# Fourteen filling products on TensorE ahead of the decoder of a four-layer conditioned network

## What is computed

```python
U = (mu @ W_dec + b_dec).reshape(B, IN_DIM + 1, K)      # mu 128x128, K = 30
param = jnp.einsum('bik,kj->bij', U, V)
weight, bias = param[:, :-1, :], param[:, -1, :]
x = x + jnp.einsum('bsd,bde->bse', x, weight) + bias[:, None, :]
x = x + clip(dcoefs * ((x * styles) @ weight.T) + bias)          # layer 1
x = x + relu(x @ w_down) @ w_up + x                              # layer 2, per entry
x = x + mlp_ln(concat(six normalised or shifted copies of x))    # layer 3
```

## Time and profile before

| | |
|---|---|
| three runs, median | 525.68 us |
| lowest and highest | 521.61 and 526.17 us |
| the profiled execution | 521.21 us |
| its span, first to last instruction | 519.4 us |
| mean granted clock of TensorE | 0.994 |

### The profile page before, as it was taken

The page is one execution under the profiler, slowest core; times in us unless marked ns, Lnnn a source line. Parts: engine busy times, 40 slices in busy tenths (PEclk is TensorE's granted clock), DMA queues, the critical chain, the costliest instruction groups (busy, mean ns, idle before and its releaser), DMA issues.

```text
span 519.4 us, 9425 instructions
## 1 busy us (share of the span) xinstructions
PE 486.3 (94%) x3198; PEld 354.2 (68%) x3198; DVE 405.8 (78%) x696; ACT 336.3 (65%) x638; POOL 391.0 (75%) x367
## 2 busy tenths in 40 slices
PE   2987887999999999999999999999999999998993
PEld 2953644767677776768686867677776768687682
DVE  2958876868788788888787878788787888886863
ACT  4573667456767676766777776767676767656832
POOL 6468799889878879697978787788779793787321
PEclk9999999999999999999999999999999999999997
DMA  8887705625252352608080716253442613104102
GB/s 299 247 304 208 203 20 124 163 73 135 83 127 81 77 171 56 191 24 223 0 229 17 205 43 173 74 136 112 106 142 63 175 47 90 49 21 145 40 2 81
DMA packets 34989, 61.78 MB, mean 119 GB/s; under 512 B 5017, under 2 KB 17413, under 8 KB 34580
## 3 DMA queue, kind: packets, MB, share of 16 engines
q1 hardware_dynamic: 28756, 43.98, 30.2%
q0 software_dynamic: 5344, 16.87, 11.3%
q10 hardware_dynamic: 864, 0.61, 0.4%
HBM read 52.58 MB, written 8.87 MB: 118 GB/s over the span
## 4 chain that ended last, share of the span: by engine, by line
PE 79%; POOL 6%; DVE 5%; DMA 4%; issue 3%; ACT 2%; SPq 0%; DVEq 0%; POOLq 0%; ACTq 0%
PE ps_c L902 11%; PE ps_c L904 11%; PE ps_c L903 10%; PE ps_d L948 9%; PE ps_d L962 5%; PE ps_a L976 5%; PE ps_b L902 3%; PE ps_b L903 3%; PE ps_b L904 3%; PE ps_b L935 2%; PE ps_a L988 2%; DMA set_wdec<-in_nets_rows 2%; PE ps_a L994 2%; PE ps_b L994 2%; DMA set_wdec<-in_W_dec 1%
## 5 line engine op out<-in xcount | busy, mean ns | idle before, releaser
L1507 POOL DMA_INDIRECT pw_rows<-in_pw,gidx x64 | 65.0, 1016 | 17.9 <-issue 17.4
L948 PE MATMUL ps_d<-xm_t,l_w 128*128 128x512 f32 x128 | 59.0, 603 | 2.2 <-POOL xm_t L1516 2.2
L1209 ACT ACTIVATE h<-h,nb_h,rstd_h 128x256 f32<-128x256 f32 x64 | 33.3, 591 | 33.1 <-POOL nb_h L1531 33.0
L1240 ACT ACTIVATE tm_t_h<-ps_a 128x1024 fp32r<-128x1024 f32 x16 | 16.4, 1026 | 45.6 <-DVE ps_a L1413 45.6
L1516 POOL TENSOR_TENSOR xm_t<-x_t,style 128x1024 f32<-128x1024 f32 x16 | 30.5, 1905 | 20.2 <-DVE x_t L1345 20.1
L948 PEld LDWEIGHTS ps_d<-xm_t,l_w 128*128 128x128 f32 x128 | 23.1, 190 | 26.8 <-issue 24.2
L1546 POOL TENSOR_TENSOR h<-xhat,pw_rows 128x1024 f32<-128x1024 f32 x16 | 38.0, 2378 | 4.1 <-ACT xhat L1209 4.1
L1565 POOL TENSOR_TENSOR w_up<-up_rep,ugub 128x1024 f32<-128x1024 f32 x16 | 38.0, 2372 | 2.2 <-issue 2.0
L1551 POOL TENSOR_TENSOR h<-h,pw_rows 128x1024 f32<-128x1024 f32 x16 | 38.3, 2394 | 1.3
L1567 POOL TENSOR_TENSOR w_up<-w_up,ugub 128x1024 f32<-128x1024 f32 x16 | 38.1, 2382 | 1.3
L902 PE MATMUL ps_b<-w_h,act_t_l 128*128 128x256 f32 x128 | 37.7, 294 | 0.4 <-DVE act_t_l L1450 0.4
(11 more groups left out here) (251 smaller groups left out, 1551.2 us busy)
## 6 DMA issues: line engine op xcount, KB each, us to landing
ugub<-ugub_scratch SPq DMA_DIRECT2D x32, 512.0 KB, 6.8
x_t<-in_x_t SPq DMA_DIRECT2D x16, 512.0 KB, 5.7
out<-y_out SPq DMA_DIRECT2D x15, 512.0 KB, 7.3
set_wdec<-in_W_dec SPq DMA_DIRECT2D x2, 1920.0 KB, 9.6
set_wdec<-in_int_W SPq DMA_DIRECT2D x1, 1536.0 KB, 9.8
set_wdec<-in_nets_rows SPq DMA_DIRECT2D x1, 1152.0 KB, 12.2
pw_rows<-in_pw,gidx POOLq DMA_INDIRECT x64, 3.7
set_wdec<-in_nets_W SPq DMA_DIRECT2D x1, 768.0 KB, 4.8
```

Source lines behind the costliest of these rows:

```text
L948: m = eng.matmul(ps_l1[:, o, :], l1_w[:, k, o * P:(o + 1) * P], xm_t[:, k, :], start=k == 0, stop=k == KB - 1)
L1209: m = eng.activation(out[:, j, :], src[:, j, :], ACT.Identity, bias=nb[k][:, j:j + 1], scale=rstd[k][:, j:j + 1])
L1507: eng.indirect_dma_start(pw_rows[c.ring][:, j, :], None, t["pw"], bass.IndirectOffsetOnAxis(ap=gidx[c.ring][:, j:j + 1], axis=0)).then_inc ...
```

## The change

A fifth place for `pe_warm` is put in front of the decoder, with fourteen products into bank 0 of ps_b, and waits only for the ones. The memset of the ones is taken out of `g_init` and made GpSimd's first work as `g_ones`; all five places now wait for z_pool at 1. The arguments of the other four places are the same, in a table.

```diff
+        WARM = ((z_pool, 1, ps_b, 0, 14), (c_ug, 1, ps_d, 0, 13), (v_dca, 1, ps_a, 0, 13), (v_x1, 2, ps_b, 0, 7),
+                (v_x1, 2, ps_b, 0, 13))
...
         def pe_warm(eng, c):
-            s, v, out, count = ((c_ug, 1, ps_d[:, 0, :], 13), (v_dca, 1, ps_a[:, 0, :], 13),
-                                (v_x1, 2, ps_b[:, 0, :], 7), (v_x1, 2, ps_b[:, 0, :], 13))[c.n]
-            eng.wait_ge(z_pool, 5)
+            s, v, ps, k, count = WARM[c.n]
+            eng.wait_ge(z_pool, 1)
             eng.wait_ge(s, v)
             for _ in range(count):
-                eng.matmul(out, ones[:, :], ones[:, :].unsqueeze(1).broadcast_to([P, CH // P, P]), start=True, stop=True)
+                eng.matmul(ps[:, k, :], ones[:, :], ones[:, :].unsqueeze(1).broadcast_to([P, CH // P, P]), start=True, stop=True)
...
+        def g_ones(eng, c):
+            eng.memset(ones[:, :], 1.0).then_inc(z_pool, 1)
 
         def g_init(eng, c):
...
-            eng.memset(ones[:, :], 1.0).then_inc(z_pool, 1)
...
-                      begin=[(pe_dec, 0), (pe_tail, 0), (pe_dec, 1), (pe_dec, 2), (pe_dec, 3), (pe_dec, 4),
+                      begin=[(pe_warm, 0), (pe_dec, 0), (pe_tail, 0), (pe_dec, 1), (pe_dec, 2), (pe_dec, 3), (pe_dec, 4),
...
-                      begin=[(g_init, 0), (g_b2rows, 0), (g_dcoef, 0), (g_style, 0), (g_gather, 0), (g_moroot, 0),
+                      begin=[(g_ones, 0), (g_init, 0), (g_b2rows, 0), (g_dcoef, 0), (g_style, 0), (g_gather, 0), (g_moroot, 0),
```

More of the change, by code:

```diff
@@ L1617, in _ @@
             run_slots(eng,
-                      begin=[(pe_dec, 0), (pe_tail, 0), (pe_dec, 1), (pe_dec, 2), (pe_dec, 3), (pe_dec, 4),
+                      begin=[(pe_warm, 0), (pe_dec, 0), (pe_tail, 0), (pe_dec, 1), (pe_dec, 2), (pe_dec, 3), (pe_dec, 4),
                              (pe_dec, 5), (pe_dec, 6), (pe_dec, 7), (pe_dec, 8), (pe_dec, 9), (pe_dec, 10),
                              (pe_dec, 11), (pe_style, 0), (pe_dec, 12), (pe_dec, 13), (pe_dec, 14), (pe_dec, 15),
-                             (pe_ug, 0), (pe_t, 0), (pe_dc, 0), (pe_hid, 0), (pe_x1, 0), (pe_warm, 0), (pe_mo, 0),
-                             (pe_l1, 0), (pe_t, 1), (pe_warm, 1), (pe_dn, 0), (pe_mot, 0), (pe_up, 0), (pe_x1, 1),
+                             (pe_ug, 0), (pe_t, 0), (pe_dc, 0), (pe_hid, 0), (pe_x1, 0), (pe_warm, 1), (pe_mo, 0),
+                             (pe_l1, 0), (pe_t, 1), (pe_warm, 2), (pe_dn, 0), (pe_mot, 0), (pe_up, 0), (pe_x1, 1),
                              (pe_cls, 0), (pe_x3r, 0), (pe_row, 0), (pe_l1, 1), (pe_xht, 0), (pe_t, 2),
-                             (pe_warm, 2), (pe_dn, 1), (pe_warm, 3), (pe_up, 1), (pe_x1, 2), (pe_x3r, 1),
+                             (pe_warm, 3), (pe_dn, 1), (pe_warm, 4), (pe_up, 1), (pe_x1, 2), (pe_x3r, 1),
                              (pe_cp, 0), (pe_t, 3), (pe_l1, 2), (pe_shift, 0), (pe_tm, 0), (pe_hht, 0), (pe_dn, 2),
```

## The result

Twenty executions of each kernel: 524.58 us median with the change (521.81 to 527.28), 521.37 without (520.05 to 526.17). The ratio is 1.0043, with a 95% interval of 1.0025 to 1.0062. By this interval the changed kernel is slightly slower. The medians themselves lie 3.2 us apart. The three runs that stood ahead of the prediction had put the kernel before at 525.68, near the upper end of its spread. So 525.4 as a time came near by luck, from a start 4.3 us too high, and -0.3 as a change had the wrong sign: it is +2.2 by the ratio (0.43% of 521.4).

The account below looks back on a forecast made before the run. The prediction took TensorE as the bound, busy 94% of the span and carrying 79% of the chain. From the 525.68 us median it took -0.3, the clock being low again at the decoder, giving 525.4, range 519.0 to 526.9.

Parts of the forecast that it names:

- -0.3 as a change: Expected change of the whole time, with bounds -0.5 and +0.25, the clock falling back before or just into the decoder.
- The clock: On TensorE before the decoder: it falls back in the 2.4 to 3.6 us gap or shortly after 9.47; chance 0.60.
- My bound of 0.5 us for the gain: In the decoder: if the clock falls only after 9.47, each us of full clock saves half, at most about 0.5.
- Rival A: At the gap before the decoder: the clock survives, gain 2.2 us, 523.5 against the median; chance 0.30.
- The step that failed: At the decoder's end: an earlier sixteenth `m_dec` moves three waiting loads and everything behind; full value 2.2 us.
- point (2): Fourteen products on TensorE before the decoder, ending at 5.9 to 7.1, delay nothing by themselves; 2.2 us of cover.
- Rival B: Starved stretch from 47.6 to 54.2: the clock falls there in more executions, costing 2.75 us, 528.4; chance 0.07.

Follow-up runs that it names:

- e3_fill2: The changed kernel with 20 instead of 13 filling products in front of the first pe_dn; 523.89 us, ratio 1.0027.
- e8_rows_first: The changed kernel with load_rown issued before load_w1; 527.03 us, ratio 1.005.
- e9_wide4: The changed kernel with four float32 products in place of the fourteen and three in place of the thirteen before pe_mo; 520.66 us, ratio 0.9971.
- e12_wide5_2: As e9_wide4, but five float32 products in front of the decoder and two in front of pe_mo; 522.21 us, ratio 0.9968.
- e7_shift80: The changed kernel with eighty more products of 8 columns behind the fourteen; 525.11 us, ratio 1.002.
- e1_bridge22: The changed kernel with 22 instead of 14 products in front of the decoder; 523.17 us, ratio 1.0017.
- e10_wide6: As e9_wide4, but six float32 products in front of the decoder; 523.89 us, ratio 1.0033.
- e6_after: The changed kernel again with no edit, in the second session; 525.19 us, ratio 1.0009.
- e5_small14: The kernel before with GpSimd's ones first and fourteen products of 8 columns in front of the decoder; 525.7 us, ratio 1.003.
- e2_ones_only: The changed kernel without the fourteen products, only GpSimd's ones coming first; 522.44 us, ratio 0.9993.

## Why the prediction was wrong, and where it was right

**The clock: right.** The fourteen products ran from 1.08 at 0.43 each, the clock rose during them, they ended at 6.6 (5.9 to 7.1 forecast), and it fell back in the gap or just behind it in every profile with a gap of 2.8 us or more: at 9.0 to 9.4 in the changed kernel, e3_fill2 and e8_rows_first, at 11.01 and 10.86 in e9_wide4 and e12_wide5_2. It fell at 10.62 in e7_shift80 too, with a gap of 1.85 us and eighty small products ahead of it. With 0.94 us (e1_bridge22) or hardly any (e10_wide6) it was kept. The rule of the Trainium skill on idle stretches ("TensorE: Matmul & The Clock Gate", section "Why this matters for your kernels") would have let the clock stand in the shortest of these; the measurements side with the earlier trace rows. My bound of 0.5 us for the gain was too low: since the clock fell at 9.27 it could be back at 12.68 instead of 14.98, and the decoder ended 1.06 earlier in this pair. It doesn't always (27.17 in e6_after), and it varies in the kernel before as well, 25.85 to 26.73 in three profiles.

**Rival A's first half: right.** A decoder at full rate ends at 24.6 and 24.7 (e1_bridge22, e10_wide6), where 24.5 had been worked out from VectorE's chain.

**The step that failed** is the one all of the sum leant on: "whatever makes the sixteenth `m_dec` come earlier moves these loads, and through them everything behind". The issue moves, the bulk of the pieces moves, but the load is over when its last piece is, and one DMA engine's share was held up. That the end follows the landing (span = landing + 479.0 to 479.7 in eight of the profiles) made this step the one that decided in them; the other five have later falls of the clock, which add 1.1 to 4.2 us. The 2.2 us that rival A gained in the decoder became ratios of 1.0017 and 1.0033 in the two kernels that did realise it. What the load did instead: it landed 15.2 and 16.0 us after the decoder's end in the changed kernel's two profiles, against 13.4 to 13.7 in the three of the kernel before.

**The cost that was missing** stands in point (2): the products "delay nothing by themselves". That is true of TensorE's time. They are also 28 instructions in a stream that is read in blocks of 16,384 bytes, and with them in it the second block was read at 35.6 instead of 46.8. The view that would have warned was there, DMA queue 8 in the part on DMA queues: one packet at 26.8, one at 46.8, with the longest DMA wait of the chain between them. I did not ask when they came.

That the queue is TensorE's I conclude from its moving with TensorE's count of instructions alone (e5_small14, e9_wide4 and e10_wide6), and from the distances: in the kernel before, the packets at 435.06, 457.28 and 479.90 lie 256 and 258 of TensorE's records apart (products, weight loads and the sequencer's). The place of the second block differs as well: TensorE had started 546 to 557 records when it was read in the kernel before (three profiles), e2_ones_only, e9_wide4 and e12_wide5_2, and 434 to 468 in the changed kernel (twice), e1_bridge22, e3_fill2, e5_small14, e8_rows_first and e10_wide6. That is about a hundred records earlier, for 10 to 44 instructions more, so it is no plain shift by their number. The Trainium skill ("Advanced Engine Details and Errata", section "ISA Cache") gives a cache line of 16 KB, 256 instructions, which the 16,384 bytes of the packet agree with. The Trainium skill also says ("Trainium Kernel Development and Optimization", section "Key Constraints") that DMAs issued from SyncE, ScalarE and GpSimd run on the same sixteen engines and interleave; of the reading of instructions it says nothing there. That the packet of 1.07 us takes its turn on one of these engines, too, is what the stragglers of nets_rows suggest.

**Rival B** (slower, by falls of the clock in the starved stretch) had the right sign, and more to it than its 0.07. In the profiles of the changed kernel and e1_bridge22 the falls at 50 came and cost nothing (landing + 479.15 and + 479.1); in the changed kernel VectorE was busy for 3.16 of 3.30 us there. Falls further on did cost, as the last section lists. And most executions without a profile had more of them, by their clock. With the fall in the gap and the one after the last product alone, as in e9_wide4's profile, the mean granted clock is 0.991. It lies at 0.978 to 0.990 in all twenty executions of the changed kernel, and at 0.991 or above in ten of e9_wide4's twelve. The changed kernel's seven executions at 0.988 and 0.990 took 521.8 to 524.2 us, the thirteen below 523.0 to 527.3. So part of the 2.8 us by which its median lies above its profiled execution goes with further falls. That the late landing brings them about, by starving TensorE longer, would fit e9_wide4, but no run tests it by itself.

**What stays open.** How much of 0.43% is the change: its second copy measured 1.0009, and copies of the kernel before differ by 0.4%. What sets the moment of the reading is not settled; e2_ones_only shows one at 33 without any added instruction. Its share in the executions that were not profiled is not known either, nor how what they lost divides between the landing and the falls of the clock. The two versions with nearly the old number of instructions are the only edited ones whose interval lies below 1 (0.9971 and 0.9968, both just under it). That is no larger than the difference between copies, and I do not claim it as shown.

## What to carry to other kernels

Filling products need not be free on an idle engine: they are instructions, and the blocks in which instructions are read are DMA traffic. Before adding some to a stream, look up when the instruction queues' packets fall in the trace of before, and keep them out of a load that the chain waits for; fewer, longer products (float32, 512 columns) do the same work for the clock. And follow a saving past the point where it is made: a load that is issued a microsecond earlier is only worth what its last piece does. Look at the mean granted clock of all executions as well: here the one profiled was the shortest of twenty, and it showed fewer falls than most.

## What the runs showed that I had not expected

- With one packet of 16,384 bytes, some 1.1 us long, read between 27 and 39, a load of 128 pieces landed 1.5 to 3.5 us later (15.2 to 16.9 against 13.4 to 13.7 after the decoder's end): its last pieces of 9216 bytes took 0.4 to 0.84 us instead of 0.35. Why they slow down is not shown; the loads issued behind, x_t and ugub, are under way by then and may share the engine.
- A fall of the clock costs by its place. With none between the decoder and the last products the span is the landing + 479.0 to 479.3 (the kernel before three times, e9_wide4). With one at 50.2 to 50.7 it is + 479.1 to 479.5 (the changed kernel, e1_bridge22, e3_fill2), with one of 6.83 us from 47.98 + 479.7 (e10_wide6). Later ones cost more: at 52.94 + 480.2 (e5_small14), at 56.8 + 480.6 (e2_ones_only), at 54.99 + 481.8 (e7_shift80), and at 478.49, in the drained pipeline near the end, + 481.6 (e12_wide5_2). E6_after, with falls at 56.8 and 483.46, has + 483.2.
- The same kernel, profiled three times, had its clock rise at 14.98, 13.06 and 13.51, and a decoder's end between 26.73 and 25.85: a spread of 0.9 us in the very term that the change aims at.
